# First ramp of a macaron block on one core: two weight loads on another queue, four weight pieces scaled on another engine, and two steps moved

## What is computed

```python
def fp4_quant_dequant(x):                 # blocks of 16 along the last dim
    scale = jnp.maximum(jnp.max(jnp.abs(xb), -1, keepdims=True) / 6.0, 1e-12)
    idx = jnp.searchsorted(_MID, jnp.abs(xb / scale))
    return (_GRID[idx] * jnp.sign(xb) * scale).reshape(shape)

def fp4_linear(x, w):
    return jnp.einsum('bsk,nk->bsn', fp4_quant_dequant(x), fp4_quant_dequant(w))

def ffn(x):                               # H = 256, I = 704
    return fp4_linear(silu(fp4_linear(x, w_gate)) * fp4_linear(x, w_up), w_down)

x = x + 0.5 * ffn(layernorm(x))
x = x + attention(layernorm(x))           # Wq, Wk, Wv, Wo with biases
x = x + 0.5 * ffn(layernorm(x))
```

## Time and profile before

| | |
|---|---|
| median of 3 runs | 961.54 us (959.61 to 961.99) |
| the profiled execution | 962.39 us, its span 960.5 us |
| granted TensorE clock, mean of the span | 0.991 |
| TensorE busy | 912.7 us, 95% |
| VectorE busy | 708.7 us, 74% |
| ScalarE busy | 655.1 us, 68% |
| GpSimd busy | 495.1 us, 52% |

### The profile page before, as it was taken

One profiled execution on the slowest core, in us unless ns is written; L12 is line 12 of the kernel. 1 busy time (PEld: TensorE's weight loads), 2 busy tenths in 40 slices (PEclk: granted clock), 3 DMA queues, 4 the chain that ended last, 5 costly groups with the idle time before them and its releaser, 6 DMA issues.

```text
span 960.5 us, 16316 instructions
## 1 busy us (share of the span) xinstructions
PE 912.7 (95%) x5704; PEld 814.4 (85%) x5704; DVE 708.7 (74%) x1163; ACT 655.1 (68%) x1368; POOL 495.1 (52%) x557
## 2 busy tenths in 40 slices
PE   3889999999989999999989999999988999999997
PEld 2678888888888789998988889998877888998987
DVE  7888988897757666655563554545586999999997
ACT  5767778888865485767664586767783687656654
POOL 3445667666520064545654064544576566665652
PEclk9899999999999999999999999999999999999999
DMA  9100000000000000000000000000000000000001
GB/s 321 38 1 1 1 1 1 2 1 1 1 1 2 0 2 1 1 1 2 1 1 1 1 1 1 1 2 1 1 1 1 1 23 24 23 23 23 2 23 44
DMA packets 11554, 13.83 MB, mean 14 GB/s; under 512 B 849, under 2 KB 10577, under 8 KB 11473
## 3 DMA queue, kind: packets, MB, share of 16 engines
q1 hardware_dynamic: 11472, 12.79, 3.9%
HBM read 8.59 MB, written 4.19 MB: 13 GB/s over the span
## 4 chain that ended last, share of the span: by engine, by line
PE 81%; DVE 11%; ACT 4%; issue 3%; DMA 0%; POOL 0%; SPq 0%; DVEq 0%; ACTq 0%; POOLq 0%
PE bank L1658 22%; PE bank L1899 17%; PE bank L1561 6%; PE bank_b L1669 6%; PE bank L1936 4%; PE bank L1940 4%; PE bank L1938 4%; PE bank_b L1676 4%; PE bank L1862 2%; PE bank L1697 2%; PE bank_b L1940 1%; PE bank_b L1936 1%; PE bank_b L1938 1%; DVE rounded L736 1%; PE bank L1880 1%
## 5 line engine op out<-in xcount | busy, mean ns | idle before, releaser
L551 POOL TENSOR_TENSOR p_lo<-s_ring,p_hi 128x512 fp32r<-128x512 f32 x128 | 165.7, 1299 | 234.5 <-ACT p_hi L1412 234.2
L513 POOL TENSOR_TENSOR zq<-grid,s_neg 128x256 f32<-128x256 f32 (+2 forms) x184 | 172.7, 963 | 46.2 <-DVE grid L742 46.2
L902 DVE TENSOR_TENSOR top<-bank,top 128x512 f32<-128x512 f32 x112 | 77.4, 691 | 130.0 <-ACT s_ring L1396 129.9
L1658 PE MATMUL bank<-w_hi,T_hi 128*128 128x512 f32 (+1 forms) x384 | 150.9, 393 | 6.3 <-DVE z L701 5.6
L1658 PE MATMUL bank<-w_hi,T_lo 128*128 128x512 f32 (+1 forms) x384 | 145.1, 378 | 0.0
L1658 PE MATMUL bank<-w_lo,T_hi 128*128 128x512 f32 (+1 forms) x384 | 144.9, 377 | 0.0
L1396 ACT ACTIVATE s_ring<-bank 128x512 f32<-128x512 f32 x128 | 76.1, 594 | 85.7 <-PE bank L1899 85.5
L1238 ACT ACTIVATE T_hi<-bank 128x1024 fp32r<-128x1024 f32 (+1 forms) x68 | 64.7, 952 | 78.0 <-PE bank L1561 77.9
L1936 PE MATMUL bank<-v_hl,p_hi 128*128 128x258 f32 x384 | 110.7, 288 | 2.0 <-POOL p_lo L551 2.0
L1940 PE MATMUL bank<-v_hl,p_lo 128*128 128x258 f32 x384 | 108.6, 283 | 0.0
L1938 PE MATMUL bank<-v_hl,p_hi 128*128 128x256 f32 x384 | 108.6, 283 | 0.0
(11 more groups left out here) (221 smaller groups left out, 2296.8 us busy)
## 6 DMA issues: line engine op xcount, KB each, us to landing
out<-x SPq DMA_DIRECT2D x7, 512.0 KB, 2.9
x<-in_L_attn_hidden_states SPq DMA_DIRECT2D x3, 1024.0 KB, 14.1
x<-in_L_attn_hidden_states SPq DMA_DIRECT2D x2, 512.0 KB, 7.4
wraw<-in_L_ffn_w_down SPq DMA_DIRECT2D x1, 704.0 KB, 8.2
wraw<-in_L_ffn_w_gate SPq DMA_DIRECT2D x1, 640.0 KB, 4.4
wraw<-in_L_ffn_w_up SPq DMA_DIRECT2D x1, 640.0 KB, 6.1
wq_s<-in_L_attn_Wq SPq DMA_DIRECT2D x1, 512.0 KB, 8.2
wk_s<-in_L_attn_Wk SPq DMA_DIRECT2D x1, 512.0 KB, 8.4
```

What stands on the lines that cost most here:

```text
L513: last = nc.gpsimd.tensor_tensor(out=blocks(zq[:, to:to + hi - lo]), in0=blocks(grid[:, lo:hi]), in1=spread(s_neg[:, par, lo // BLOCK:hi / ...
L551: nc.gpsimd.tensor_tensor(out=lower_buf(n, c), in0=score_buf(n, c), in1=upper_buf(n, c).bitcast(F32), op=ALU.subtract).then_inc(plo_done, 1)
L902: nc.vector.tensor_tensor(out=top[:], in0=score_bank(c), in1=other, op=ALU.max).then_inc(top_done, 1)
L1658: last = nc.tensor.matmul(gu[:, lo:hi], lhsT=T[:, par, HK + kd, :], rhs=w[:, kd, lo:hi], start=n == 0, stop=n == len(terms) - 1)
```

## The change

1. The two 64 KB loads are issued by ScalarE, at the start of its program, on a semaphore of their own (`mixed_in`). VectorE waits for the large gate load, reduces piece 0, waits for `mixed_in`, and reduces piece 1.
2. ScalarE runs a one-column Silu on a constant before its first copy.
3. `weight_y` of pieces 1, 2, 4 and 5 is on GpSimd (semaphore `y_pool`, and a table `Y_MADE` that says which semaphore to wait on); pieces 0 and 3 stay on VectorE. GpSimd makes 1 and 2 ahead of `weight_q(0)`, 4 behind the bias broadcast, 5 behind zq of step -3. `weight_scales` of the second pair is ahead of `weight_grid(0)`.
4. On VectorE `product(0)` is ahead of `weight_grid(4)`.
5. On ScalarE x_means 1 is behind normalise 0, x_variances 1 ahead of weight_abs 4, and both woT_out ahead of chain_rest -3.
6. `query_bias` goes into step -2: on TensorE behind the transposes of that step and so behind gate/up 1, and on ScalarE ahead of nv_upper; both halves of the nv product stand behind chain_lower of that step, and both halves of Wo's transposes ahead of chain_lower -3.

```diff
@@ SyncE
-            sp.dma_start(wraw[0:HR, 5 * D:6 * D], w_gate[5 * P:I, :]).then_inc(gate_in, 16)
-            sp.dma_start(wraw[HR:P, 5 * D:6 * D], w_up[0:P - HR, :]).then_inc(gate_in, 16)
@@ GpSimd
+            def weight_y(i):
+                pool.wait_ge(wc["inv"], i // 2 + 1)
+                if i >= 2:
+                    pool.wait_ge(wc["abs"], i - 1)
+                    pool.wait_ge(wc["rnd"], i - 1)
+                nc.gpsimd.tensor_tensor(out=blocks(wy[:, i % 2, :]), in0=blocks(wraw[:, i * I:(i + 1) * I]),
+                                        in1=spread(wsm[:, 3, i * HB:(i + 1) * HB], HB),
+                                        op=ALU.mult).then_inc(wc["y_pool"], 1)
...
             first_ffn, second_ffn = ffn_step(0), ffn_step(1)
+            pool.wait_ge(wc["y"], 1)
+            weight_y(1)
+            weight_y(2)
             weight_q(0)
             group_std(0)
             for i in (1, 2, 3):
                 weight_q(i)
             first_ffn(-5, 1)
             broadcast_biases()
+            weight_y(4)
             first_ffn(-4, 0)
+            weight_y(5)
             group_std(1)
             weight_q(4)
@@ VectorE
+                if first == 0:
+                    nc.vector.tensor_reduce(out=wsm[:, 0, 0:HB], in_=blocks(wraw[:, 0:I]), axis=AX_X,
+                                            op=ALU.max, apply_absolute_value=True)
+                    dve.wait_ge(mixed_in, 16 * 2)
+                    nc.vector.tensor_reduce(out=wsm[:, 0, HB:2 * HB], in_=blocks(wraw[:, I:2 * I]), axis=AX_X,
+                                            op=ALU.max, apply_absolute_value=True).then_inc(wc["amax"], 1)
...
-            dve.wait_ge(gate_in, 16 * 3)
+            dve.wait_ge(gate_in, 16)
             weight_scales(1, 0, 2)
             weight_y(0)
-            weight_y(1)
-            weight_grid(0)
             dve.wait_ge(up_in, 16)
             weight_scales(2, 2, 4)
+            weight_grid(0)
             weight_grid(1)
-            weight_y(2)
             weight_y(3)
...
             weight_scales(3, 4, NW)
-            weight_y(4)
             first_blocks(-4, 0)
+            first_product(0)
             weight_grid(4)
-            first_product(0)
-            weight_y(5)
             first_blocks(-3, 1)
@@ ScalarE
+            act.dma_start(wraw[0:HR, 5 * D:6 * D], w_gate[5 * P:I, :]).then_inc(mixed_in, 16)
+            act.dma_start(wraw[HR:P, 5 * D:6 * D], w_up[0:P - HR, :]).then_inc(mixed_in, 16)
+            act.wait_ge(half_set, 1)
+            nc.scalar.activation(warm[:], mhalf[:, 0:1], ACT.Silu)
...
                     if extra and c == -2:
+                        query_bias()
                         nv_upper()
...
             normalise(0)
+            x_means(1)
             m_upper()
...
             absolute(-3)
+            x_variances(1)
             weight_abs(4)
-            x_means(1)
             normalise(3)
-            x_variances(1)
             absolute(-2)
             silu_gate(0)
             chain_upper(-3, 1)
-            query_bias()
             woT_out(0)
+            woT_out(1)
             chain_rest(-3, 1)
-            woT_out(1)
             weight_abs(5)
@@ TensorE
                     if extra and c == -2:
-                        value_output_product(0)
+                        query_bias()
...
                     if extra and c == -2:
+                        value_output_product(0)
                         value_output_product(1)
...
             transpose_wo(0)
-            query_bias()
+            transpose_wo(1)
             chain_lower(0, -3, 1)
-            pe.wait_ge(aw["bq_s"], 2)
-            transpose_wo(1)
             rounds(0, -2)
```

## The result

The changed kernel took 963.92 us (median of 6 runs, 961.61 to 964.49) against 961.44 (6 runs) for the kernel before: ratio 1.0029, 95% interval 1.0018 to 1.0040. Run again beside its variants it took 963.85 (11 runs), ratio 1.0024 (1.0011 to 1.0037). It is slower, by about 2.5 us, where about 2 faster was forecast; 963.9 lies above the forecast's range of 957.5 to 962.6.

What follows compares the result with a forecast made beforehand. TensorE was taken to bound the kernel (95% busy), only the ramp changing, bound by VectorE, ScalarE, then VectorE. Both ways to the reduction end near 49.25; 7.84 more gives the anchor at 57.1, 2.2 earlier: median 959.4 us, range 957.5 to 962.6.

Steps and rivals of the forecast that it cites:

- the anchor: First matmul of gate/up of tile 3 on TensorE, opening its full rounds; forecast to move from 59.30 to 57.1 us.
- VectorE's way: VectorE's chain from Silu 0 through product 0, grids and steps -3 and -2 to the reduction behind normalise 5; ends 49.05.
- TensorE's way: TensorE's chain from gate/up 1 at 37.2 through query_bias and nv products to the reduction behind normalise 5: 12.05, ending 49.25.
- rival 2: Clock falls once, near gate/up 1, which then costs 6.0 instead of 3.95; gain 0.2, 961.3 us; chance 0.27.
- rival 3: Clock falls before 37.2, query_bias keeps it down, slowing nv products and gate/up; anchor 2.9 later, 964.4 us; chance 0.06.
- gate/up 3.95 at 2.4 GHz: TensorE's gate/up 1 taken at full clock: 3.95 us, against 6.0 at the old clock.
- the two nv products 3.5: TensorE's two nv products behind query_bias, taken at 2.4 GHz: 3.5 us.
- One for one: Whole kernel's time moves by exactly what the anchor at 59.30 moves: 2.2 earlier.
- The loads: Small loads on ScalarE's queue land by 5.2 and 5.75, no later than 6.26; VectorE starts 1.0 earlier (0 to 1.2).
- The shared port: VectorE operations with two SBUF operands and GpSimd products exclude each other; y of step -2 ends 32.6 to 34.6, 33.8 taken.
- Rival 1: VectorE wins the port every time: y of step -4 at 20.0, of step -2 at 32.6; gain 3.4, 958.1 us; chance 0.16.
- rival 4: No effect: small loads late, y4 and y5 on GpSimd delay y of step -2 to 36.0; 961.5 us; chance 0.09.

Runs made afterwards that it cites:

- the bias and the loads put back: Changed kernel with query_bias (all of part 6) and the two small loads back in their old places; 959.69 us, ratio 0.9986 to the kernel before.
- the bias put back: Changed kernel with all of part 6 undone, query_bias again ahead of gate/up 1; 960.61 us, ratio 0.9998 to the kernel before.
- a wide bias: Changed kernel with the 24 one-column query_bias matmuls made 128 columns wide; 961.83 us, ratio 1.0012 to the kernel before.
- the bias behind nv: Changed kernel with query_bias behind the two nv products on TensorE and behind normalise 5 on ScalarE; 961.52 us, ratio 1.0008 to the kernel before.
- part 6 alone: Kernel before with only part 6 of the change added; 966.66 us, ratio 1.0067 to the kernel before.
- the extra matmuls: Changed kernel with the third part of gate/up 2 computed twice, ahead of gate/up 3; 961.46 us, ratio 1.0007 to the kernel before.

## Why the prediction was wrong

**What held.** The order of bounds: from the start of normalise 0 to that of the last T_lo ScalarE took 10.30 (19.05 to 29.35; 10.75 forecast), gate/up 1 came 2.3 behind Silu 0 (2.45), the anchor 7.85 behind the reduction (7.84). The table load is gone. With the bias and the loads put back the front is as forecast: normalise 0 at 17.73 (17.65) and T_lo at 28.06 (28.4). Each of the two ways to the reduction is confirmed by a variant. VectorE's way, from Silu 0 on, took 13.98 with the bias put back (35.30 to 49.28; 14.30 forecast). TensorE's way, from gate/up 1 on, took 12.38 with a wide bias and no fall of the clock (37.77 to 50.15; 12.05 forecast).

**The step that failed** is the choice of the forecast against rivals 2 and 3: the terms of TensorE's way "gate/up 3.95 at 2.4 GHz" and "the two nv products 3.5", put in with no price for the clock. The nv products took 5.30 and 6.50 in the two profiles of the changed kernel. I gave rival 3, the bias keeping the clock down, 0.06, and made it hang on a fall before 37.2. In the second profile rival 2 came too, and later than it was said to: the clock fell at 38.8, in gate/up 1, and was back at 42.3. But rival 3 needs no such fall: in the first profile gate/up 1 ran at full clock and the clock fell behind the one-column matmuls all the same, at 46.5. Rival 3 asked whether the clock would have risen again by 43; the question was what the moved matmuls do to it. A ramp without any fall, as the forecast had it from 37 on, is rare besides: of the sixteen profiles only two have none, both with the wide bias. The prediction also read the old fall as 38.5; it was at 38.1, 1.6 behind TensorE's last matmul and not 2.0.

**One for one.** "The time moves by what 59.30 moves" left out that the first full round can be at 1.2 GHz too: the second fall added 1.5 between gate/up 3 and Silu of tile 3. The profile of the kernel before does not show it; five of the other fifteen do: the changed kernel's two, the bias put back, the bias behind nv, and part 6 alone. Why some have it and some not stays open.

**The loads.** Forecast 1.0 earlier, with 0 as the worst. DMA issues of the changed kernel (as rows 5):

```profile
wraw<-in_L_ffn_w_gate ACTq DMA_DIRECT2D x1, 64.0 KB, 4.5
wraw<-in_L_ffn_w_up ACTq DMA_DIRECT2D x1, 64.0 KB, 6.3
```

The second took 6.3 us to land instead of 4.5, beside the up load, which is now issued 1.2 earlier and moves 640 KB. The scales were ready at 9.53, not 8.0 as forecast; before it was 8.95. The bound failed since it took the old landing for the worst case. By a sentence of the Trainium skill (DMA: Bandwidth & Descriptors, Issuing engines are not separate DMA queues) transfers from two issuing engines run on the same DMA engines and interleave; the longer landing beside the up load agrees with it, and with the loads back in their old order the wait is gone, though no run moves the up load alone. That only the sequencer's time is saved was still too kind here: time was lost. Cost: 0.4 to 1.4 at gate/up 0, about 1.0 in the mean of the profiles, where the forecast had nothing to lose.

**The shared port.** Both engines took turns as forecast, one VectorE operation longer by 0.75 to 1.04 each time: y of step -4 (1.30), rounded -3 (1.18), y of step -2 (1.30), s_up of step -1 (1.21). Rounded and grid of step -3 ended at 32.30, behind both ends that the prediction gave (31.0 and 31.75), and y of step -2 at 34.66, its worst case of 34.6, where it took 33.8. Rival 1 did not come. The Trainium skill (SBUF — State Buffer, Who interferes with whom) says that the instruction issued later is blocked for the whole of the other one; the four rows agree, each ending 0.04 to 0.29 us behind the end of GpSimd's product. That pieces 4 and 5 can cost more than they give was in the prediction as the worse end for y of step -2 and, with the late small loads, as rival 4, which had this y at 36.0 and a chance of 0.09: both of its causes came, and neither in that size.

**The waits.** TensorE waited 0.47 for zq of step -2, which the sum did not have. The query bias itself was in the sum, with 2.85 (it took 2.74).

In sum, for the profiled execution, against the forecast's reduction at 49.25: 0.67 from the front, 0.47 for zq, 1.7 for the clock in the nv products, less 0.15 over the other terms, are 51.94; 1.5 more for the second fall make 4.2. The forecast for this execution was 960.2, it took 964.0: 3.8, since about 0.3 is won back between Silu of tile 3 and the end. Another execution of the same kernel has the low clock in other places, so these shares are those of one profile.

## What to carry to other kernels

A step that runs in an engine's wait costs nothing, and the same step moved behind that wait can cost its whole length (the rest rose by 3.1 with part 6 alone, and fell by 1.6 when part 6 was undone in the changed kernel): ask of every moved step which wait it leaves, before asking what its absence lets through. On TensorE ask too what the moved matmuls are like: narrow ones ahead of wide ones can cost by the clock about as much as by their own time (1.7 and 2.9 in the nv products of two profiles, against 2.7). And a load taken out of an ordered queue loses its place: the old landing time is no bound for the new one.

## What the runs showed that I had not expected

Twenty-four matmuls of one column (2.74 us, TensorE counted as busy throughout) directly behind 4 us of full gate/up matmuls at 2.4 GHz were followed by 1.2 GHz within about a microsecond of their end; the same with 128 columns were not, in the one profile of it. It is no rule without exception: with the extra matmuls the one-column bias stood in the same place, and the clock held. A busy TensorE in the profile is therefore no sign that the clock will hold. Executions of one kernel differ by 4 us and more, in part with the granted clock: six executions are few for a difference of 2 us.
